# Gated experts: two experts of 176 rows as three chunks of 128, with a chunk shared by halves

## The reference, cut to what matters

```python
# x_flat: 8192 tokens x 128; E = 8 experts, I = 176, shared expert of 352
logits = x_flat @ gate_w.T
scores = softmax(logits);  w = scores * (one of the 2 largest)
g, u = gate and up parts of x_flat @ experts_gate_up[e].T      # 176 + 176 per expert
expert_out[e] = (silu(g) * u) @ experts_down[e].T
out = sum_e w[e] * expert_out[e]
shared = (silu(x @ shared_gate_w.T) * (x @ shared_up_w.T)) @ shared_down_w.T
x = x + out + sigmoid(x @ shared_expert_gate_w.T) * shared
```

## Time and profile before

| | |
|---|---|
| median of 3 runs | 4117.2 us (4113.91 to 4119.01) |
| the profiled execution | 4117.64 us, its span 4115.9 us |
| granted TensorE clock, mean of the span | 0.956 |
| busy in the span | PE 3653.7, PEld 3001.4, DVE 2844.3, ACT 1929.6, POOL 1099.0 us |
| L1175 with downT (the outputs of this stage) | 2560 MATMUL records, 311.5 us busy |
| L1287, h of this stage | 240 instructions, 165.2 us busy |

### The profile page before, as it was taken

How to read it: one execution, slowest core, us unless ns; L and a number is a source line. 1 busy time by engine, 2 the same in 40 slices (tenths; PEclk the granted TensorE clock), 3 DMA queues, 4 the chain that set the end, 5 groups by cost and what they waited for, 6 DMA issues and landing times. The chain is left out here.

```text
span 4115.9 us, 108620 instructions
## 1 busy us (share of the span) xinstructions
PE 3653.7 (89%) x42378; PEld 3001.4 (73%) x42378; DVE 2844.3 (69%) x6136; ACT 1929.6 (47%) x4763; POOL 1099.0 (27%) x1214
## 2 busy tenths in 40 slices
PE   5999699978887788789999988869999997999999
PEld 4887688876666644478887865548887886888888
DVE  5777555559999899856665668876665665666665
ACT  2454455547777744345555531115554553323232
POOL 1222133332222233212222223322222221232322
PEclk9999899989999999989999998889999998999999
DMA  1000000000000000000000000000000001000000
GB/s 68 9 9 6 24 0 0 0 10 9 10 9 9 7 1 0 4 24 6 8 6 8 6 9 0 0 22 6 8 6 9 6 6 31 1 10 10 0 10 11
DMA packets 14699, 39.25 MB, mean 10 GB/s; under 512 B 3277, under 2 KB 4749, under 8 KB 12814
## 3 DMA queue, kind: packets, MB, share of 16 engines
q1 hardware_dynamic: 14341, 33.95, 2.7%
HBM read 29.74 MB, written 4.19 MB: 8 GB/s over the span
## 5 line engine op out<-in xcount | busy, mean ns | idle before, releaser
L641 ACT ACTIVATE projL<-bank 128x512 f32<-128x512 f32 (+1 forms) x640 | 373.3, 604 | 714.7 <-PE bank L126 698.9
L464 POOL TENSOR_TENSOR probL<-probL,invL 128x1024 f32<-128x1024 f32 x160 | 304.7, 1904 | 1274.6 <-DVE invL L723 1274.6
L1153 POOL TENSOR_TENSOR accM<-accM,partM 128x512 f32<-128x512 f32 x272 | 347.6, 1278 | 816.2 <-DVE partM L1255 814.8
L1226 ACT ACTIVATE siluM<-bank 120x512 f32<-120x512 f32 x240 | 143.5, 598 | 456.4 <-PE bank L126 456.2
L321 ACT ACTIVATE probL<-bank,neg_maxL 128x64 f32<-128x64 f32 x1024 | 304.9, 325 | 110.0 <-PE bank L285 107.5
L545 PE MATMUL bank<-valuesL,probTL 64*64 64x128 f32 x10240 | 321.0, 275 | 13.1 <-ACT probTL L651 13.1
L545 PEld LDWEIGHTS bank<-valuesL,probTL 64*64 64x64 f32 x10240 | 282.0, 134 | 68.9 <-issue 54.2
L720 DVE TENSOR_REDUCE totalL<-probL 128x16 f32<-128x1024 f32 x160 | 194.9, 1218 | 196.6 <-ACT probL L656 196.4
L712 DVE TENSOR_REDUCE neg_maxL<-bank 128x16 f32<-128x1024 f32 x160 | 195.9, 1224 | 187.4 <-PE bank L564 142.8
L1175 PEld LDWEIGHTS bank<-downT,hM 120*128 120x128 f32 x2560 | 310.5, 192 | 15.0
L1175 PE MATMUL bank<-downT,hM 120*128 120x128 f32 x2560 | 311.5, 275 | 0.0
(11 more groups left out here) (253 smaller groups left out, 8990.0 us busy)
## 6 DMA issues: line engine op xcount, KB each, us to landing
ct0L<-in_ctxP SPq DMA_DIRECT2D x24, 192.0 KB, 2.4
ct1L<-in_ctxP SPq DMA_DIRECT2D x24, 192.0 KB, 3.1
x<-in_x SPq DMA_DIRECT2D x4, 1024.0 KB, 8.8
out<-x SPq DMA_DIRECT2D x4, 1024.0 KB, 3.9
nct<-in_ctxT SPq DMA_DIRECT2D x16, 192.0 KB, 2.5
w_natural<-in_L0w SPq DMA_DIRECT2D x2, 1152.0 KB, 8.7
downT<-in_L3down SPq DMA_DIRECT2D x1, 1200.0 KB, 11.9
gateT<-in_L3gate SPq DMA_DIRECT2D x1, 900.0 KB, 4.7
```

The lines of the kernel that those rows point to most:

```text
L464: nc.gpsimd.tensor_tensor(segments(prob[:, slot, :]), segments(prob[:, slot, :]), per_segment(inv[:, slot, :]), ALU.mult).then_inc(prob_re ...
L641: nc.scalar.activation(proj[:, u, :], rot.bank(step, f"P{u}")[0:rows, :], ACT.Copy, scale=scale if paired and u % 2 == 0 else 1.0).then_in ...
L1153: nc.gpsimd.tensor_tensor(acc[:, :, :], acc[:, :, :], part[:, ex % 2, :, :], ALU.add)\
```

## The change

Each pair of experts gets chunks of 128 rows: chunk 3p has the first 128 rows of the first expert, 3p + 1 the first 128 of the second, and chunk 3p + 2 the last 48 of the first in its rows 0 to 47 and the last 48 of the second in rows 64 to 111, zeros between. The number of chunks and the products stay; F is 128. The output of both experts of a pair is made in one go, `output_pair`: for each token tile t a full matmul for each expert into its own bank, then two matmuls of 64 rows of contraction, one in each half of the shared chunk. Both outputs stand 2 chunks behind chunk 3p + 2, so that the even expert's is made a chunk later than before; DVE's `add` of the even expert moves by a chunk too, and both adds of a pair stand one behind the other. `h` has 6 buffers, three for a pair's chunks, in turn. downT has 15 blocks of 128 rows instead of 20 of 120.

```diff
-    def first_chunk(self, ex):
-        return 3 * (ex // 2) + ex % 2 if self.paired else 2 * ex
+    def last_chunk(self, ex):
+        return 3 * (ex // 2) + 2 if self.paired else 2 * ex + 1

     def experts_at(self, n, behind):
         return [(back, ex) for back in (1, 0) for ex in range(self.E)
-                if self.first_chunk(ex) + 1 + behind == n + back * self.C]
+                if self.last_chunk(ex) + behind == n + back * self.C]
...
-        NH = next(s for s in (4, 5, 6) if {0, 1}.isdisjoint({n % s for n in range(self.first_chunk(E - 2), C)}))
+        NH = 6 if self.paired else next(
+            s for s in (4, 5, 6) if {0, 1}.isdisjoint({n % s for n in range(2 * (E - 2), C)}))
+
+        def kept(n, slot):
+            return (n // 3 + slot) % 2 * 3 + n % 3 if self.paired else n % NH
...
+                def output_pair(i, ex, slot):
+                    n, half = 3 * (ex // 2), P // 2
+                    pe.wait_ge(h_ready, i * C + n + 3 + NB)
+                    pe.wait_ge(Y_read, i * E + ex + NY)
+                    for t in range(G):
+                        tok, out = slice(t * P, (t + 1) * P), slice(t * D, (t + 1) * D)
+                        for e in range(2):
+                            nc.tensor.matmul(y_bank[e][:, out], h[:, kept(n + e, slot), tok], W2[:, n + e, :],
+                                             start=(t == 0), stop=False, skip_group_check=True)
+                        for e in range(2):
+                            rows = slice(e * half, (e + 1) * half)
+                            last = nc.tensor.matmul(y_bank[e][:, out], h[rows, kept(n + 2, slot), tok],
+                                                    W2[rows, n + 2, :], start=False, stop=(t == G - 1),
+                                                    skip_group_check=True)
+                            if t == G - 1:
+                                last.then_inc(Y_done, 1)
+
+                def outputs(i, n, slot, first):
+                    for back, ex in self.experts_at(n, 2):
+                        if back and first or self.paired and ex % 2:
+                            continue
+                        (output_pair if self.paired else output)(i - back, ex, 1 - slot if back else slot)
...
-                        for back, ex in self.experts_at(n, 2):
-                            if not (back and first):
-                                output(i - back, ex)
+                        outputs(i, n, slot, first)
...
-                            nc.vector.tensor_tensor(h[:, n % NH, :], up_bank[n % NB][0:F, :], silu[:, n % NB, :],
+                            nc.vector.tensor_tensor(h[:, kept(n, slot), :], up_bank[n % NB][0:F, :], silu[:, n % NB, :],
                                                     ALU.mult).then_inc(h_ready, 1)
...
-    E, F, C = 10, 120, 15
+    E, F, C = 10, 128, 15
...
-        W1, U1, W2 = sb("gateT", [P, C, F]), sb("upT", [P, C, F]), sb("downT", [F, 2 * E, D])
+        W1, U1, W2 = sb("gateT", [P, C, F]), sb("upT", [P, C, F]), sb("downT", [F, C, D])
...
+    def chunks(rows):
+        rows = rows.reshape(5, 2, 176, D)
+        out = np.zeros((5, 3, 128, D), np.float32)
+        out[:, 0:2] = rows[:, :, 0:128]
+        out[:, 2, 0:48], out[:, 2, 64:112] = rows[:, 0, 128:], rows[:, 1, 128:]
+        return out.reshape(15, 128, D)
```

More of the change, by code:

```diff
@@ L1106, in run @@
         nc = c.nc
-        C = self.C = self.first_chunk(E - 1) + 2
+        C = self.C = self.last_chunk(E - 1) + 1
         NB = 3
-        NH = next(s for s in (4, 5, 6) if {0, 1}.isdisjoint({n % s for n in range(self.first_chunk(E - 2), C)}))
+        NH = 6 if self.paired else next(
+            s for s in (4, 5, 6) if {0, 1}.isdisjoint({n % s for n in range(2 * (E - 2), C)}))
+        def kept(n, slot):
+            return (n // 3 + slot) % 2 * 3 + n % 3 if self.paired else n % NH
         NY = 2
@@ L1164, in _, with output @@
                 prepare_pe(pe)
-                def output(i, ex):
-                    n = self.first_chunk(ex)
+                def output(i, ex, slot):
+                    n = 2 * ex
                     pe.wait_ge(h_ready, i * C + n + 2 + NB)
@@ L1175, in output @@
                             last = nc.tensor.matmul(y_bank[ex % NY][:, t * D:(t + 1) * D],
-                                                    h[:, (n + j) % NH, t * P:(t + 1) * P],
+                                                    h[:, kept(n + j, slot), t * P:(t + 1) * P],
                                                     W2[:, 2 * ex + j, :], start=(t == 0 and j == 0),
@@ L1211, in _ @@
                     for back, ex in self.experts_at(n, 2):
-                        if back:
-                            output(NG - 1, ex)
+                        if back and not (self.paired and ex % 2):
+                            (output_pair if self.paired else output)(NG - 1, ex, 1)
             @block.scalar
@@ L1228, in group @@
                         else:
-                            nc.scalar.activation(h[:, n % NH, :], gate_bank(n, slot)[0:F, :], ACT.Silu,
+                            nc.scalar.activation(h[:, kept(n, slot), :], gate_bank(n, slot)[0:F, :], ACT.Silu,
                                                  scale=row_scale[:, n:n + 1]).then_inc(h_ready, 1)
@@ L2021, in lay_out, with both @@
     gu = a["L3_ffn_experts_gate_up"].reshape(8, 2, 176, D)
[L2023 to L2028, removed]
-    down = np.concatenate([a["L3_ffn_shared_down_w"].T, a["L3_ffn_experts_down"].transpose(0, 2, 1).reshape(-1, D)])
[L2030 to L2034, removed]
+    def chunks(rows):
[4 more added lines that the diff above has]
+        return out.reshape(15, 128, D)
+    def both(shared, routed):
+        return chunks(np.concatenate([shared, routed.reshape(-1, D)])).transpose(2, 0, 1)
+    o["L3gate"] = both(a["L3_ffn_shared_gate_w"], gu[:, 0])
+    o["L3up"] = both(a["L3_ffn_shared_up_w"], gu[:, 1])
+    down = np.concatenate([a["L3_ffn_shared_down_w"].T, a["L3_ffn_experts_down"].transpose(0, 2, 1).reshape(-1, D)])
+    o["L3down"] = chunks(down).transpose(1, 0, 2)
     o["L3router"] = np.concatenate([a["L3_ffn_gate_w"], a["L3_ffn_shared_expert_gate_w"]]).T
```

## The result

The changed kernel takes **4274.2 us** (median of 4 runs, 4267.84 to 4279.14) against 4116.4 us (median of 4, 4113.91 to 4119.01) on the same chip: a ratio of **1.0382, 95% interval 1.0364 to 1.0400**. It is slower, as forecast, but by 158 us instead of 109, and 24 us above the top of the range (4195 to 4250). The profiled execution took 4267.84 us, its span 4266.1 us at a mean granted clock of 0.943 (before 0.956).

What follows compares the result with a forecast made beforehand. PE's stream of matmuls was taken as the bound; 4117.6 + 54 (shape changes) + 42 (pause) + 10 (clock) + 1.7 (tail) = 4225.7, predicted as 4226 us, range 4195 to 4250.

Steps and rivals of the forecast that it cites:

- PE is the bound, and the change is slower: Gated experts' stage: PE's matmul stream sets the time; the changed kernel takes 4226 us, 2.6% slower.
- A: Rival: shape changes cost, but the group boundary's stall is hidden, under 0.5 us; 4174 us, chance 0.14.
- B: Rival: full-width row halves don't change the array shape, so PE keeps the saving; 4102 us, chance 0.11.
- C: Rival: row halves don't change the array shape and the boundary is hidden; 4048 us, chance 0.04.
- D: Rival: shape changes cost and the two halves run one behind the other; 4296 us, chance 0.07.
- Shape changes, +54 us: PE's pair outputs: 640 array shape changes at 0.19 us each outweigh the saved slots, +54 us in place of -71.5.
- 71.5 us: PE's pair outputs: saving from 12 slots instead of 16 a pair, if halves run side by side and nothing else changed.
- The pause, +42 us: Group boundaries: PE waits for DVE's h(2), 2.8 us at each of 15, shown as 2.57 in the record.
- the chain of steps given: Boundary: from the burst's last record, x starts at +4.06 us, h(2) ends at +7.04, PE starts at +7.21.
- The clock, +10 us (0 to 26): Behind boundary pauses: a low clock follows 0.4 of 15, losing 1.7 us of PE's time each.
- the tail of +1.7 us: End of the stage: x starts at +4.06 instead of +2.36, +1.7 us, all on the path.
- The head of -0.1: Start of the stage: weight transfers scaled by bytes, -0.5 us, and DVE's four splits behind them, +0.4.

Runs made afterwards that it cites:

- e7: Changed kernel, halves still interleaved, with acc doubled and the x update with its statistics moved to n = 10 of the next group: 4171.28 us, ratio 1.0129.
- e10: Kernel before the change, with only acc doubled and the x update moved to n = 10 of the next group: 4115.83 us, ratio 0.9996.
- e8: Changed kernel with each pair's halves behind all its full matmuls, acc doubled and the x update at n = 10 of the next group: 4076.19 us, ratio 0.9898.
- e3: Changed kernel with all full matmuls of a pair first, then all halves, two shape changes a pair instead of eight: 4127.93 us, ratio 1.0027.
- e11: Changed kernel with halves interleaved only in pair 0, behind the pause, and last in pairs 1 to 4: 4185.65 us, ratio 1.0170.
- e12: Changed kernel with halves last in pair 0, behind the pause, and interleaved in pairs 1 to 4: 4200.43 us, ratio 1.0203.
- e6: Changed kernel with only the aggregation of the statistics moved behind h(2), x staying where it is: 4245.14 us, ratio 1.0310.
- e4: Changed kernel with each pair's halves behind its full matmuls, and x += acc with its statistics behind h(4): 4126.94 us, ratio 1.0015.
- e1: Changed kernel with x += acc and its statistics behind h(4) instead of ahead of h(2): 4185.49 us, ratio 1.0167.
- e5: Changed kernel with only the statistics moved from ahead of h(2) to behind it, x staying where it is: 4187.27 us, ratio 1.0171.
- e2: Changed kernel with the shared chunk as full 128-row matmuls against zero-padded down blocks, so no shape changes: 4179.68 us, ratio 1.0148.
- e9: Changed kernel with halves last, double acc and update at n = 10, but the first expert's four halves before the second's: 4117.44 us, ratio 0.9998.

## Why the prediction failed in size

**PE is the bound, and the change is slower**: right. Rivals A, B and C (a hidden boundary, a change without a price) fall with the records of the result: 0.20 us between shapes, and a pause at every boundary. D falls with the halves 0.007 us apart.

**Shape changes, +54 us**: right. e7 against e10 gives 53, a pair 4.14 us where I had 4.25, and the price of 0.19 us a change, taken from three places in other stages, came out as 0.194. The Trainium skill's page "TensorEngine Tiling (Array Packing)", Key Properties, has the drain without a figure; these runs put 0.19 us on a change, the drain and the open weight load behind it together. The halving that its Theoretical Speedup allows shows in e8's bursts, 16 half records in eight slots, and pays once the changes are few: of 71.5 us, 30 go to 160 changes at 0.19 and 41 are left; the period shows 40.

**The pause, +42 us at 2.57 in the record**: right, 2.57 to 2.59 us at nearly every boundary (2.1 at the last), and by the chain of steps given: from the burst's last record, at 3807.37, x starts 4.09 us later (forecast 4.06), h(2) ends at 7.06 (7.04) and PE starts at 7.20 (7.21). e3's periods without a low clock, 40.29, against e8's 37.53 give 2.76 us for it, where I had 2.8. What was missed is that the last group has one of its own, 1.41 us.

**The clock, +10 us (0 to 26)**: this is the step that failed. "I take 0.4 of 15 boundaries" at 1.7 us: the low clock followed all 15, and cost about 4.1 us each, 61 in all. Both factors were wrong. The chance came from two pauses in another stage, one with and one without, too few for it. The trace of before had more: of the pauses of 2.2 to 3.1 us behind a full clock, 5 of 14 were followed by a low clock in that stage (L1570), but 13 of 14 in the stage of L1791, and there five of the 13 stretches lasted 6.8 us. One of them (PE in order of time, then the stretch behind it):

```profile
2495.91 2.08 PE L1791 MATMUL bank<-kw,xT 128*128 128x512 f32 x2 [2.86 <-DVE chosen L1894]
...
2496.00:2500.00 4.00, 4.00 (x13) 2.97 (x14) 3.87 (x9) 0.00 (x0) 1.28 (x2) 0.50 0.00 0
```

So the share doesn't go by the pause's length alone, and rows for a chance near 1 and for a longer stretch stood in the trace of before. The size came from the length of that one stretch, four microseconds, and this was the greater error, since it put even the upper bound of 26 too low: the stream behind that pause was another one. Behind the pauses here stands an output with eight changes of shape, and e11 against e3, and e12 against the changed kernel, show that this is what makes 3.4 us into 6.8 to 10.2. With 61 in place of 10 the sum is 4277, less 3 for the head: the median is 4274. (The profiled run has 4268: 6 us less in stages that the change doesn't touch.)

The Trainium skill's "TensorE: Matmul & The Clock Gate", Part 1, gives the lower level as the one of an idle or cold engine. The traces agree that it stands behind idle time: with no pause (e7, e8) the clock stayed full. On how long a pause has to be, the measurement decides: 1.80 us were followed by the low clock 13 times in 15 (e6) and 2.08 us 10 times (e4), 0.90 us at no boundary (e1 and e5). The last group's 1.41 us were followed by it in one run of twelve, e12, where the outputs behind it ran at 0.50.

**Edges**: the tail of +1.7 us was +1.4. The head of -0.1 was -3.2: I scaled the transfer by its bytes (below).

**Still open**: what decides whether a pause of 2.57 us is followed by the low clock. It did in all 15 of e2, in 7 of e3, at every second boundary, and in 5 of e12, at every third. No run tells why. Nor does one tell why changes of shape prolong it. The two halves of the 0.19, the drain and the open weight load, were not tried apart; only their sum is shown.

## What to carry to other kernels

Matmuls on half the array pay when they are grouped: here the two changes of a return trip cost 0.39 us, and two half matmuls side by side (four fp32 records) save two slots of 0.11, so eight halves between two changes win (0.89 us against 0.39) and two lose (0.22). Price a pause of PE with the clock behind it, and look at what PE does in the microseconds after it; a pause of two or three microseconds can cost more in clock than in itself. Work that a second buffer can take off the boundary (here a second `acc`, and the update nine chunks later) may be worth nothing in the old kernel (e10) and still be what the new one needs (e8 against e3, 52 us).

## What the runs showed of the hardware

- The low clock's length depends on what follows: behind equal pauses of 2.57 us it was 3.4 us, where it came, with equal full records or grouped halves (e2, e3, e12), and 6.8 to 10.2 us with a change of shape every four records (changed kernel, e11), although PE was busy all the time (11.00 of 11.00 us in e11's stretch).
- Row halves of two experts written one after the other in the stream overlap in part: 16 records took 13 slots in e9, 8 in e8 (1.44 and 0.89 us from first to last start).
- This stage's down transfer, the third in its queue, was slower to 120 partitions than its bytes say: 1200 KB landed in 11.9 us (12.2 in e10), 960 KB to 128 partitions in 8.4, and e2's 1280 KB, more bytes, to 128 in 9.3:

```profile
downT<-in_L3down SPq DMA_DIRECT2D x1, 1280.0 KB, 9.3
```
